# The first attention's output projection and the norm behind it, taken in two token halves that are set into the work around them

## The chip, the cores and the metric

The kernel runs on one core of one Trainium2 chip. The metric is the device time of one execution in microseconds (us). The core has a matmul engine (TensorE, PE; its weight loads are shown as PEld), VectorE (DVE), ScalarE (ACT), GpSimd (POOL) and SyncE (SP), which here issues all transfers. Each engine works through its own list of instructions strictly in order and waits on semaphores.

## The reference

Two transformer-like layers over 1024 tokens (`x`, 256 wide), cut to their structure:

```python
x = x + 0.5 * L0_ffn(layernorm(x))    # gate/up/down weights rebuilt from splines, silu(gate)*up
x = x + L0_attn(layernorm(x))         # 32 heads of 8, RoPE, banded bias, causal, softmax offset, @ Wo.T
x = x + 0.5 * L0_ffn(layernorm(x))    # the same weights again
x = x + 0.5 * L1_ffn(layernorm(x))    # ternary weights, rms norm inside
x = x + L1_attn(layernorm(x))         # 16 heads of 128 in 4 groups, causal
x = x + 0.5 * L1_ffn(layernorm(x))
return x
```

The change lies where the first attention ends and the second `L0_ffn` begins:

```python
out = einsum('bhij,bhjd->bhid', p, v) / denom[..., None]
out = out.transpose(0, 2, 1, 3).reshape(B, S, Dm)
return out @ Wo.T
```

## The kernel before

The order of work is written out by hand, once for each engine: `ffn(0)`, `qkv`, `attention`, `attention_out`, `norm(2)`, `ffn(1)`, `ffn(2)`, `grouped` (the second attention), `norm(5)`, `ffn(3)`. `X` holds the residual, tokens on partitions in eight blocks `tb`; `xn` holds the normed tokens, and during the first attention its output before the projection. `lnH` and `lnL` hold the transposed tokens as a high and a low part of float32 in a rounded format, since a product of full precision is made of three passes (`PASSES3`: high by high, high by low, low by high). PSUM has eight banks of 128 x 512 float32.

The attention takes 8 groups of 4 heads. Group g has 12 units (`UNITS2`): units 0 to 3 are for the first 512 queries, 4 to 11 for the others, each against one block of 128 keys. In a unit PE makes the scores (`look2`, L1274, in banks 2, 3, 4, 6), adds the band (`look2_bands`, L1291), makes the values of the unit before (`values`, L1311, bank 7), and ScalarE exponentiates (L936). In all groups but the last, PE also makes maxima for later groups (`look1`, L1229). After each half a group's output is copied to `oS` (`output_copy`), transposed back (`outputs`, L1320) and divided into `xn` by VectorE (L1763 to L1768). For the last group the first half's output is turned in unit 5, the second's after the last unit.

Then follows `attention_out`: all of `xn` is transposed (`transposed`, L1107, banks 0 to 3), ScalarE copies the high parts (L820), VectorE subtracts the low parts (L1602), PE makes 48 products with `WOA` (L1077), VectorE adds them to `X` (L1790). Around this stand six transpositions of the next layer's quantised weights (`quant_turn`, L1387), which ScalarE copies out. `norm(2)` takes statistics (L1578, L1581, L1583), GpSimd the power -0.5 (L696), VectorE scales (L1588), PE transposes again (L1107), and again high and low parts are made.

`ffn(1)` has 16 steps, eight for each token half: step t makes gate and up for 128 of 1024 inner features (`gate_up`, twelve products of 512 columns, banks 4 to 7) and then `down(t - 2)` (six products, L1171, banks 0 and 1 for the first half, 2 and 3 for the second). The first half needs only the first half's `lnH` and `lnL`. The hook `side` puts other work behind a step. After step 10 the first half's sum is copied out, and a norm follows that is already made by halves:

```python
                    if NORM_AFTER[f] is not None and t == AT_TURN:
                        norm_half(NORM_AFTER[f], 0)
                    if side:
                        side(t)
```

The queries of groups 1, 4 and 7 lie in the same memory as `lnH`, so `lnH` can't be written before the last group's scores are made. The transfers of the output weights of the second attention (`w_dense`, L680) wait on SP for `x_new` of the whole first attention.

## Time and profile before

| | us |
|---|---|
| median of 3 runs | 1083.94 |
| lowest, highest | 1083.74, 1088.75 |
| profiled execution, its own time | 1085.72 |
| its span, first to last instruction | 1083.9 |
| mean granted clock of PE | 0.962 of 2.4 GHz |

The profile is of one execution. The page gives sums; the timeline gives instructions in order of time, merged where the same form repeats (x16), with the idle time of the engine before it and what ended it in square brackets. Ends of matmuls are modelled: the start of the next instruction tells more than the length of one. L numbers are lines of the kernel before.

### The profile page before, as it was taken

The numbers are of one execution on the slowest core, as the hardware profiler recorded it, in microseconds if no ns is written. First come the engines' busy times: TensorE is split into PE (matmuls) and PEld (weight loads), VectorE is DVE, ScalarE is ACT, GpSimd is POOL, SyncE is SP. The second block draws the span as 40 slices with busy tenths as digits, with TensorE's granted clock in tenths as the row PEclk, the third lists the DMA queues.
The fourth block names the chain that finished last, engine by engine and source line by source line (L and its number), as shares of the span: only waits on it lengthen the run. The fifth ranks groups of instructions, "written<-read, shape, count | busy, mean of one in ns | idle before, by whom it ended". The sixth has DMA issues, their size and how long they took to land. (4 is left out here: it accounts for less than half of the span.)

```text
span 1083.9 us, 20902 instructions
## 1 busy us (share of the span) xinstructions
PE 976.4 (90%) x7872; PEld 669.5 (62%) x7896; DVE 751.0 (69%) x1865; ACT 577.4 (53%) x1167; POOL 398.9 (37%) x261
## 2 busy tenths in 40 slices
PE   4999677999999998989989879999999999999697
PEld 3787423333444343678867657777777777777585
DVE  7756976889888982254577657767777776777644
ACT  6442403666766677543355446555556555555264
POOL 3011220045423550000045036555656555566155
PEclk9999857999999999989989999999999999999899
DMA  4020434235532401022010000000000000000001
GB/s 108 1 81 27 153 66 85 45 71 95 97 71 62 95 23 60 1 78 78 1 40 0 1 1 1 2 1 2 2 2 2 2 2 2 1 2 2 1 1 40
DMA packets 25182, 37.94 MB, mean 35 GB/s; under 512 B 3000, under 2 KB 20904, under 8 KB 23560
## 3 DMA queue, kind: packets, MB, share of 16 engines
q1 hardware_dynamic: 25080, 36.59, 14.4%
q8 instruction: 63, 1.03, 0.4%
q14 instruction: 39, 0.32, 0.1%
HBM read 30.53 MB, written 5.85 MB: 34 GB/s over the span
## 5 line engine op out<-in xcount | busy, mean ns | idle before, releaser
L812 POOL TENSOR_SCALAR P<-P,rec 128x1024 f32<-128x1024 f32 (+7 forms) x128 | 220.1, 1724 | 177.2 <-DVE rec L1858 177.2
L936 ACT ACTIVATE PT<-bank 128x512 f32<-128x512 f32 (+2 forms) x320 | 153.0, 552 | 86.8 <-PE bank L1291 80.4
L1717 DVE CUSTOM_DVE_ANT_0 bank<-bank,stripS 128x128 f32<-128x128 f32 (+1 forms) x224 | 129.3, 606 | 29.3 <-PE bank L1229 29.3
L1443 PE MATMUL pair<-KH,QH 128*128 128x512 f16 (+3 forms) x576 | 116.1, 329 | 16.5 <-ACT P L1005 13.8
L1005 ACT ACTIVATE P<-pair,nm 128x1024 f32<-128x1024 f32 (+7 forms) x128 | 95.5, 746 | 56.0 <-DVE nm L1837 56.0
L1484 PE MATMUL bank<-PT,VH 128*128 128x128 f16 x1728 | 117.2, 219 | 0.1
L1229 PE MATMUL bank<-KT,QT 96*128 96x128 bf16 (+1 forms) x336 | 104.4, 338 | 10.5 <-DVE MX L1717 5.4
L1484 PEld LDWEIGHTS bank<-PT,VH 128*128 128x128 f16 x1728 | 107.0, 98 | 2.9 <-DVE PT L1866 0.2
L1866 DVE TENSOR_TENSOR PT<-bank,PT 128x384 f16<-128x384 f32 (+1 forms) x192 | 99.7, 547 | 11.6 <-ACT PT L820 11.6
L1274 PE MATMUL bank<-QT,KT 128*128 128x512 bf16 (+3 forms) x360 | 93.2, 326 | 13.7 <-ACT PT L936 5.6
L1632 DVE TENSOR_TENSOR hf<-sil,bank 128x512 f32<-128x512 f32 x64 | 44.0, 687 | 88.8 <-PE bank L1077 66.1
L1833 DVE TENSOR_REDUCE mx<-pair 128x1 f32<-128x1024 f32 (+7 forms) x128 | 95.8, 748 | 10.7 <-PE pair L1445 10.7
L820 ACT ACTIVATE PT<-bank 128x384 f16<-128x384 f32 (+1 forms) x192 | 86.6, 488 | 18.0 <-PE bank L1472 17.1
L696 POOL TENSOR_TENSOR rstd<-veps,mhalf 128x4 f32<-128x4 f32 x12 | 12.7, 1061 | 225.9 <-DVE veps L1583 225.9
L1472 PE MATMUL bank<-ident,P 128*128 128x128 f32 x576 | 85.7, 275 | 5.6 <-POOL P L812 5.3
L861 ACT ACTIVATE sil<-bank 128x512 f32<-128x512 f32 x64 | 38.3, 598 | 97.8 <-PE bank L1077 97.4
L1077 PE MATMUL bank<-lnH,W 128*128 128x512 f32 x256 | 86.7, 401 | 3.0 <-DVE W L1570 3.0
L1229 PEld LDWEIGHTS bank<-KT,QT 96*128 96x128 bf16 x336 | 29.2, 98 | 89.0 <-DVE MX L1717 47.2
L1443 PEld LDWEIGHTS pair<-KH,QH 128*128 128x128 f16 x576 | 47.6, 98 | 56.3 <-ACT P L1005 24.5
L1311 PE MATMUL bank<-PT,V 128*32 128x512 f32 (+3 forms) x768 | 79.6, 489 | 0.3 <-ACT PT L936 0.3
L1472 PEld LDWEIGHTS bank<-ident,P 128*128 128x128 f32 x576 | 64.6, 141 | 17.4 <-POOL P L812 8.4
L1274 PEld LDWEIGHTS bank<-QT,KT 128*128 128x128 bf16 x384 | 34.3, 98 | 53.6 <-ACT PT L936 33.4
(181 smaller groups left out, 1951.1 us busy)
## 6 DMA issues: line engine op xcount, KB each, us to landing
KT<-qk_dram SPq DMA_DIRECT2D x21, 192.0 KB
stripS<-band_rows SPq DMA_DIRECT2D x28, 128.0 KB, 3.0
qk_dram<-parts SPq DMA_DIRECT2D x12, 256.0 KB, 2.3
stripT<-seq_dram SPq DMA_DIRECT2D x27, 88.0 KB, 8.6
q_raw<-w_gu SPq DMA_DIRECT2D x4, 512.0 KB, 10.7
w_raw<-w_dense SPq DMA_DIRECT2D x2, 1024.0 KB, 7.0
w_raw<-w_q SPq DMA_DIRECT2D x2, 1024.0 KB, 5.5
QT<-qk_dram SPq DMA_DIRECT2D x14, 128.0 KB
```

What stands on the lines that cost most here:

```text
L812: pool.tensor_scalar(rows, rows, rec1[:, m % 4:m % 4 + 1], None, ALU.mult).then_inc(s["pn"], 1)
L936: act.activation(PT[:, n % 4, hs[0]:hs[-1] + 1, 0:ni], src, ACT.Exp).then_inc(s["s2_exp"], 1)
L1005: act.activation(P1[:, n % 3, 0:P * (ib + 1)], pair[n % 2][:, 0:P * (ib + 1)], ACT.Exp, bias=nm1[:, n % 2:n % 2 + 1], scale=SCALE1, accum_ ...
L1077: ins = pe.matmul(out, lhs(l, k), rhs(r, k), start=first and i == 0, stop=last and i == len(todo) - 1)
L1229: pe.matmul(ring_bank(use)[:, 0:nj], queries(g)[0:ROWS, h, P * ib:P * (ib + 1)], KT3[0:ROWS, g % 3, h, j0:j0 + nj], start=True, stop=True) ...
L1274: ins = pe.matmul(score_bank(i2)[:, ni * j:ni * (j + 1)], KT3[:, g % 3, h, P * jb:P * (jb + 1)], queries(g)[:, h, i0:i0 + ni], start=(j == ...
L1443: ins = pe.matmul(out, QH1[:, h % 2, l, P * ib:P * (ib + 1)], KH1[:, r, h // (H1 // GR), HALF * c:HALF * c + nj], start=(i == 0), stop=(i ...
L1472: ins = pe.transpose(rt_bank(use)[:, P * b:P * (b + 1)], P1[:, m % 3, HALF * c + P * b:HALF * c + P * (b + 1)], ident)
L1484: ins = pe.matmul(to, VH1[:, l, jb, DH * grp:DH * (grp + 1)], PT1[:, m % 3, r, P * jb:P * (jb + 1)], start=(jb == 0 and i == 0), stop=(jb ...
L1717: dve.tensor_tensor_reduce(out, out, stripS[:, h, HALF - nj:HALF], 1.0, LOWEST, ALU.add, ALU.max, mx).then_inc(s["s1_max"], 1)
L1833: dve.tensor_reduce(mx1[:, n % 2:n % 2 + 1], pair[n % 2][:, 0:P * (ib + 1)], AX_X, ALU.max).then_inc(s["sc_mx"], 1)
L1866: dve.tensor_tensor(PT1[:, m % 3, 1, cols], rt_bank(use)[:, 0:P * nb], PT1[:, m % 3, 0, cols], ALU.subtract).then_inc(s["tp_lo"], 1)
```

## The change

The work between the last exponentials and `ffn(1)` is cut by token halves. First half: its `xn` is transposed in the last group after unit 6's scores and values, into banks 0 and 1, and its high and low parts go to `AH` and `AL` (memory of the keys of two groups that are done); 24 products with `WOA` follow in unit 7 (banks 5 and 0); VectorE adds, takes statistics in unit 7 and scales in unit 8; PE transposes for the norm after unit 11, ahead of the last values. `ffn(1)` then starts. Second half, behind its steps: step 0 the last `outputs` (bank 3), step 1 the transposition (banks 2 and 3), step 2 the 24 products, step 3 the scaling, step 4 the norm's transposition; the quantised weights are turned at steps 5 (two), 6, 7, 8 and 9, in banks 2 and 3, which `down(8)` needs from step 10 on. ScalarE's and VectorE's `layer1_weights` go from steps 3 and 6 to 5 and 8, and from 4 and 7 to 6 and 9. `lnH` is still written only after the last scores.

```diff
         stripS = z("stripS", [P, GH, HALF], F32)
+        AH, AL = (Zone(zone_kt + 2 * GH * S * i)(f"A{i}", [P, KT, S], F32R) for i in (0, 2))
         stripT = z("stripT", [ROWS, 2, GH, STRIP], BF16)
...
-        QUANT_BANKS = [6, 7, 0, 1, 2, 3]
+        OUT_BANKS = [5, 0, 2, 3]
+        QUANT_AT = {5: (0, 1), 6: (2,), 7: (3,), 8: (4,), 9: (5,)}
+        def a_turn(half):
+            return 8 + 4 * half
+        def n_turn(half):
+            return 10 + 4 * half
         QUANT_OPS = 8
...
                 RING += [("s", i, 0) for i in look1_at(g, u)] + ([turn(g, u)] if turn(g, u) else [])
-        RING += [("o", NG - 1, 1)]
         at_ring = {u: i for i, u in enumerate(RING)}
...
         def ring_bank(use):
+            if use == ("o", NG - 1, 1):
+                return bank[3]
             if use[0:2] == ("m", 0):
...
+            def turned(out, at, half):
+                for hh in range(2):
+                    act.wait_ge(s["ln_tr"], at + hh + 1)
+                    copy(out[:, hh, HALF * half:HALF * (half + 1)], bank[2 * half + hh]).then_inc(s["ln_hi"], 1)
             def transposed(i, halves=(0, 1)):
...
                             signs(g)
+                        if g == NG - 1 and u == 6:
+                            turned(AH, a_turn(0), 0)
+                turned(lnH, n_turn(0), 0)
                 output_copy(NU * NG)
...
             qkv()
+            def beside_ffn1(t):
+                if t == 1:
+                    turned(AH, a_turn(1), 1)
+                if t == 4:
+                    turned(lnH, n_turn(1), 1)
+                if t in (5, 8):
+                    layer1_weights((t - 5) // 3)
+                for c in QUANT_AT.get(t, ()):
+                    quant_out(c)
             attention()
-            transposed(2)
-            for c in range(6):
-                quant_out(c)
-            transposed(3)
-            ffn(1, side=lambda t: layer1_weights(t // 3 - 1) if t in (3, 6) else None)
+            ffn(1, side=beside_ffn1)
             finish(1, 1)
...
                     if t % MT == 0:
-                        pe.wait_ge(s["ln_lo"], 4 * TR_OF_SUB[n] + 2 * tc + 2)
+                        pe.wait_ge(s["ln_lo"], n_turn(tc) + 2 if f == 1 else 4 * TR_OF_SUB[n] + 2 * tc + 2)
+                    if f == 1 and t == 0:
+                        pe.wait_ge(s["s2_exp"], N2 * NG)
+                    if f == 1 and t == 1:
+                        pe.wait_ge(s["acc_ev"], 2 * NG)
+                        pe.wait_ge(s["x_new"], TB + 2)
                     for m, (b, name, freed) in enumerate(((4, "gate", "silu"), (6, "up", "h"))):
...
                     pe.wait_ge(s["hlo"], base + t + 1)
+                    if f == 1 and t == MT:
+                        pe.wait_ge(s["q_ev"], 6)
                     if f == 0 and t < MT and t % 2 == 0:
...
                 pe.wait_ge(s["acc_ev"], 2 * g + w + 1)
-                wait_ring(pe, use)
+                if use in at_ring:
+                    wait_ring(pe, use)
+                else:
+                    pe.wait_ge(s["s2_exp"], N2 * NG)
                 for b in range(4):
...
                         transposition(turn(g, u))
+                        if g == NG - 1 and u == 6:
+                            attention_turn(0)
+                        if g == NG - 1 and u == 7:
+                            attention_out(0)
+                norm_half(2, 0)
                 values(NU * NG - 1)
-                outputs(NG - 1, 1)
-            def attention_out():
-                pe.wait_ge(s["on"], 2 * NG)
-                for th in range(2):
-                    transposed(th)
-                quant_turn(0, 2)
-                pe.wait_ge(s["ln_lo"], 4 * 2 + 4)
-                for tb in range(TB):
-                    if tb == 4:
-                        pe.wait_ge(s["q_ev"], 2)
-                    ins = products(bank[4 + tb // 2][:, D * (tb % 2):D * (tb % 2 + 1)], lambda p, k: ln(p, k, P * tb, P),
+            def attention_turn(half):
+                pe.wait_ge(s["on"], 2 * NG - 1 + half)
+                pe.wait_ge(s["s1_max"], len(LOOK1))
+                pe.wait_ge(s["m_ev"], 2 * NG)
+                transposed(half)
+            def attention_out(half):
+                pe.wait_ge(s["ln_lo"], a_turn(half) + 2)
+                for tb in range(4 * half, 4 * half + 4):
+                    ins = products(bank[OUT_BANKS[tb // 2]][:, D * (tb % 2):D * (tb % 2 + 1)], lambda p, k: (AH, AL)[p][:, k, P * tb:P * (tb + 1)],
                                    lambda p, k: WOA[:, p, k, :], PASSES3)
...
-            def quant_turn(first, last):
-                if first == 0:
+            def quant_turn(c):
+                if c == 0:
                     pe.wait_ge(s["q_in"], 16)
-                    pe.wait_ge(s["acc_ev"], 2 * NG)
-                for c in range(first, last):
-                    dst = bank[QUANT_BANKS[c]].bitcast(BF16)
-                    for b in range(8):
-
-                        src = q_keep[:, c, D * (b % 4) + P * (b // 4):D * (b % 4) + P * (b // 4 + 1)] if c < 4 else q_keep[:, c, P * b:P * (b + 1)]
-                        ins = pe.transpose(dst[:, P * b:P * (b + 1)], src, identb[:, :])
-                    ins.then_inc(s["q_tr"], 1)
+                    pe.wait_ge(s["ln_lo"], n_turn(1) + 2)
+                if c >= 2:
+                    pe.wait_ge(s["q_ev"], c - 1)
+                dst = bank[2 + c % 2].bitcast(BF16)
+                for b in range(8):
+                    src = q_keep[:, c, D * (b % 4) + P * (b // 4):D * (b % 4) + P * (b // 4 + 1)] if c < 4 else q_keep[:, c, P * b:P * (b + 1)]
+                    ins = pe.transpose(dst[:, P * b:P * (b + 1)], src, identb[:, :])
+                ins.then_inc(s["q_tr"], 1)
+            def beside_ffn1(t):
+                if t == 0:
+                    outputs(NG - 1, 1)
+                if t == 1:
+                    attention_turn(1)
+                if t == 2:
+                    attention_out(1)
+                if t == 4:
+                    norm_half(2, 1)
+                for c in QUANT_AT.get(t, ()):
+                    quant_turn(c)
...
             attention()
-            attention_out()
-            quant_turn(2, 6)
-            pe.wait_ge(s["q_ev"], 6)
-            norm(2)
-            ffn(1)
+            ffn(1, side=beside_ffn1)
             ffn(2, side=beside_ffn2)
...
+            def turned(hi, lo, at, half):
+                cols = slice(HALF * half, HALF * (half + 1))
+                for hh in range(2):
+                    dve.wait_ge(s["ln_hi"], at + hh + 1)
+                    dve.tensor_tensor(lo[:, hh, cols], bank[2 * half + hh], hi[:, hh, cols].bitcast(F32), ALU.subtract).then_inc(s["ln_lo"], 1)
             def rms(f, tc):
...
                             group_sums(g - 1)
-                outputs(NG - 1, 1)
+                        if g == NG - 1 and u == 6:
+                            turned(AH, AL, a_turn(0), 0)
+                        if g == NG - 1 and u == 7:
+                            attention_out(0)
+                            norm_stats(2, 0)
+                        if g == NG - 1 and u == 8:
+                            norm_apply(2, 0)
+                turned(lnH, lnL, n_turn(0), 0)
-            def attention_out():
-                transposed(2)
-                for tb in range(TB):
+            def beside_ffn1(t):
+                if t == 0:
+                    outputs(NG - 1, 1)
+                if t == 1:
+                    turned(AH, AL, a_turn(1), 1)
+                if t == 2:
+                    attention_out(1)
+                    norm_stats(2, 1)
+                if t == 3:
+                    norm_apply(2, 1)
+                if t == 4:
+                    turned(lnH, lnL, n_turn(1), 1)
+                if t in (6, 9):
+                    layer1_weights(t // 3 - 2)
+            def attention_out(half):
+                for tb in range(4 * half, 4 * half + 4):
                     dve.wait_ge(s["wo_mm"], tb // 2 + 1)
-                    dve.tensor_tensor(X[:, tb, :], bank[4 + tb // 2][:, D * (tb % 2):D * (tb % 2 + 1)], X[:, tb, :], ALU.add).then_inc(s["x_new"], 1)
+                    dve.tensor_tensor(X[:, tb, :], bank[OUT_BANKS[tb // 2]][:, D * (tb % 2):D * (tb % 2 + 1)], X[:, tb, :], ALU.add).then_inc(s["x_new"], 1)
...
             attention()
-            attention_out()
-            norm(2)
-            ffn(1, side=lambda t: layer1_weights(t // 3 - 1) if t in (4, 7) else None)
+            ffn(1, side=beside_ffn1)
             ffn(2, side=beside_ffn2)
```

How the instructions stand now. PE in the last group, before: two units' scores (L1274), bands (L1291) and values (L1311), from the scores of unit 6 on.

```order
L1274 MATMUL bank<-QT_121,KT_92 128x512 x4
L1311 MATMUL bank<-PT,V_94 32x512 x4
L1274 MATMUL bank<-QT_121,KT_92 128x512 x4
L1291 MATMUL bank<-stripT,flipb 32x128 x16
L1311 MATMUL bank<-PT,V_94 32x512 x4
L1274 MATMUL bank<-QT_121,KT_92 128x512 x4
L1291 MATMUL bank<-stripT,flipb 32x256 x16
```

PE in the same place, with the change (scores L1305, bands L1322, values L1342).

```order
L1305 MATMUL bank<-QT_123,KT_92 128x512 x4
L1342 MATMUL bank<-PT,V_94 32x512 x4
L1131 MATMUL bank<-ident,xn 128x128 x8
L1305 MATMUL bank<-QT_123,KT_92 128x512 x4
L1322 MATMUL bank<-stripT,flipb 32x128 x16
L1342 MATMUL bank<-PT,V_94 32x512 x4
L1101 MATMUL bank<-WOA,A_99 128x256 x2
L1101 MATMUL bank<-WOA,A_100 128x256
...
L1305 MATMUL bank<-QT_123,KT_92 128x512 x4
L1322 MATMUL bank<-stripT,flipb 32x256 x16
```

Eight transposes of `xn` stand ahead of unit 7's scores, and behind unit 7's values 24 products with `A` (written as x2 and x1 rows, the first pair of eight is shown) ahead of unit 8's scores; the last two rows are unit 8's scores and bands.

ScalarE from the group's last exponentials to the first steps of the block, before.

```order
L936 ACTIVATE PT<-bank 128x2x256 x2
L936 ACTIVATE PT<-bank 128x2x128 x2
L820 ACTIVATE oS<-bank 128x512
L820 ACTIVATE lnH<-bank 128x512 x4
L820 ACTIVATE WGU_68<-bank 128x2x512 x4
L820 ACTIVATE WD_69<-bank 128x8x128 x2
L820 ACTIVATE lnH<-bank 128x512 x4
L861 ACT_TABLE_LOAD
L861 ACTIVATE sil<-bank 128x512 x2
```

ScalarE there, with the change (exponentials L951, copies L829, silu L876).

```order
L951 ACTIVATE PT<-bank 128x2x256 x2
L951 ACTIVATE PT<-bank 128x2x128 x2
L829 ACTIVATE lnH<-bank 128x512 x2
L829 ACTIVATE oS<-bank 128x512
L876 ACT_TABLE_LOAD
L876 ACTIVATE sil<-bank 128x512 x2
L829 ACTIVATE hH<-hf 128x512
L829 ACTIVATE A_99<-bank 128x512 x2
L876 ACTIVATE sil<-bank 128x512
```

The copies that stood between the exponentials and the first silu have gone, but for two of `lnH` and one of `oS`; two copies of `A` now follow the second silu.

VectorE between the attention and the block, before: low parts, additions to `X`, statistics, scalings, low parts.

```order
L1602 TENSOR_TENSOR lnL<-bank,lnH 128x512 x4
L1790 TENSOR_TENSOR X<-bank,X 128x256 x8
L1578 BN_STATS stats<-X 128x6 x4
L1581 BN_AGGR mv<-stats 128x2 x4
L1583 TENSOR_SCALAR veps<-mv 128x4
L1578 BN_STATS stats<-X 128x6 x4
L1581 BN_AGGR mv<-stats 128x2 x4
L1583 TENSOR_SCALAR veps<-mv 128x4
L1588 TENSOR_SCALAR xn<-X,mv,rstd 128x256 x8
L1602 TENSOR_TENSOR lnL<-bank,lnH 128x512 x4
```

VectorE with the change, steps 0 to 2 of the block (`hf` and `hL` are the block's own, L1686 and L1692).

```order
L1686 TENSOR_TENSOR hf<-sil,bank 128x512
L1817 TENSOR_TENSOR DEN<-bank,EO 128x16
L1819 RECIPROCAL REC<-DEN 128x16
L1822 TENSOR_TENSOR xn<-bank,REC 128x4x32
L1686 TENSOR_TENSOR hf<-sil,bank 128x512
L1692 TENSOR_TENSOR hL<-hf,hH 128x512
L1656 TENSOR_TENSOR A_100<-bank,A_99 128x512 x2
L1686 TENSOR_TENSOR hf<-sil,bank 128x512
L1692 TENSOR_TENSOR hL<-hf,hH 128x512
L1865 TENSOR_TENSOR X<-bank,X 128x256 x4
L1625 BN_STATS stats<-X 128x6 x4
L1628 BN_AGGR mv<-stats 128x2 x4
```

The division of the last output stands behind step 0, the low parts of `A` behind step 1, and the additions to `X` with the second half's statistics behind step 2.

## Rows read from the trace of the kernel before

**Rows 1.** The page: busy us (share of the span) xinstructions of each engine.

```profile
PE 976.4 (90%) x7872; PEld 669.5 (62%) x7896; DVE 751.0 (69%) x1865; ACT 577.4 (53%) x1167; POOL 398.9 (37%) x261
```

**Rows 2.** Busy time by engine in three stretches; the column before DMA is the granted clock.

```profile
core 0: us, PE busy (x) PEld busy (x) DVE busy (x) ACT busy (x) POOL busy (x), PEclk, DMA share, GB/s
427.90:445.90 18.00, 16.17 (x185) 5.96 (x183) 0.72 (x3) 14.36 (x30) 0.00 (x0) 1.00 0.00 1
445.90:468.20 22.30, 16.70 (x140) 15.71 (x140) 14.07 (x43) 10.39 (x14) 2.28 (x2) 0.80 0.30 95
468.20:534.80 66.60, 66.60 (x300) 55.03 (x298) 31.27 (x54) 25.54 (x41) 1.01 (x1) 0.99 0.09 32
```

**Rows 3.** Timeline (start us, us, engine, line), last group, units 7 and 8.

```profile
435.70 0.41 PE L1291 MATMUL bank<-stripT,flipb 96*32 96x128 bf16 x16
...
435.94 1.03 PE L1311 MATMUL bank<-PT,V 128*32 128x512 f32 x8
436.05 2.06 ACT L936 ACTIVATE PT<-bank 128x512 f32<-128x512 f32 x4 [0.73 <-PE bank L1291]
...
437.19 1.37 PE L1274 MATMUL bank<-QT,KT 128*128 128x512 bf16 x3 [0.22 <-ACT PT L936]
...
438.49 0.62 PE L1291 MATMUL bank<-stripT,flipb 96*32 96x256 bf16 x16
```

**Rows 4.** Timeline from the last exponentials to the second feed-forward block.

```profile
445.00 0.61 PE L1311 MATMUL bank<-PT,V 128*32 128x256 f32 x8
445.17 0.66 ACT L936 ACTIVATE PT<-bank 128x256 f32<-128x256 f32 x2 [0.34 <-PE bank L1291]
...
448.57 3.09 PE L1107 MATMUL bank<-ident,xn 128*128 128x128 f32 x16 [0.88 <-DVE xn L1768]
...
453.07 0.50 PE L1077 MATMUL bank<-WOA,lnH 128*128 128x256 f32 x2
...
458.92 1.96 PE L1387 MATMUL bank<-identb,q_keep 128*128 128x128 bf16 x32
...
461.74 1.04 POOL L696 TENSOR_TENSOR rstd<-veps,mhalf 128x4 f32<-128x4 f32 x1 [56.36 <-DVE veps L1583]
...
463.36 2.83 DVE L1588 TENSOR_SCALAR xn<-X,mv,rstd 128x256 f32<-128x256 f32 x8
...
464.88 3.65 PE L1107 MATMUL bank<-ident,xn 128*128 128x128 f32 x16 [4.00 <-DVE xn L1588]
...
468.23 0.79 PE L1077 MATMUL bank<-lnH,W 128*128 128x512 f32 x1
```

**Rows 5.** The granted clock by the microsecond.

```profile
449.00:450.00 1.00, 1.00 (x9) 1.00 (x7) 0.11 (x1) 0.61 (x2) 0.00 (x0) 0.61 0.00 0
452.00:453.00 1.00, 1.00 (x13) 0.90 (x11) 0.84 (x2) 0.74 (x2) 0.00 (x0) 0.68 0.00 0
...
462.00:463.00 1.00, 0.00 (x0) 0.00 (x0) 1.00 (x5) 1.00 (x2) 0.78 (x1) 0.94 0.96 316
...
469.00:470.00 1.00, 1.00 (x5) 0.76 (x4) 0.72 (x2) 0.98 (x2) 0.00 (x0) 0.65 0.00 0
```

**Rows 6.** Timeline, eight transposes set into feed-forward work at full clock.

```profile
519.39 1.03 PE L1136 MATMUL bank<-ident,OT 128*128 128x128 f32 x8
...
520.18 0.47 PE L1077 MATMUL bank<-lnH,W 128*128 128x512 f32 x1
...
532.56 1.04 PE L1107 MATMUL bank<-ident,xn 128*128 128x128 f32 x8
...
533.83 1.29 DVE L1602 TENSOR_TENSOR lnL<-bank,lnH 128x512 fp32r<-128x512 f32 x2 [1.09 <-ACT lnH L820]
```

**Rows 7.** Timeline of PE, second block, starts of steps 3 and 4.

```profile
478.59 0.39 PE L1077 MATMUL bank<-lnH,W 128*128 128x512 f32 x1
...
482.67 0.39 PE L1077 MATMUL bank<-lnH,W 128*128 128x512 f32 x1
```

**Rows 8.** Busy time and clock while the attention starts up.

```profile
145.00:176.00 31.00, 23.31 (x128) 7.38 (x125) 23.45 (x53) 4.06 (x6) 0.00 (x0) 0.50 0.18 33
```

2 lines of the change are left out of this document (1 added, 1 removed).

## The prediction

> **What bounds the kernel now.** I read the page's totals first, then the stretch that the change touches, then its timeline. TensorE (PE) is busy 976.4 of 1083.9 us [rows 1], so the time is PE's own work plus the 107 us in which it stands still, plus what it loses when its clock is at the lower level. A change that keeps every matmul, as this one does, can gain only from the last two.
>
> The touched stretch lies in three parts [rows 2]. In the last group's units 4 to 11 (18.0 us) PE is busy 16.2. From the last exponentials to the second feed-forward block (22.3 us) it is busy 16.7: 5.6 us are idle, and the mean granted clock is 0.80. In the block itself (66.6 us) it is busy all the time: whatever is put in there is paid in full, but nothing waits as long as other engines have their parts ready.
>
> The middle part in order of time [rows 4]: the last exponentials start at 445.17 and take 0.66, so they end at 445.83. Then come sixteen transposes (448.57, 3.09 us), two hand-over transpositions of the quantised weights, 48 output products (453.07 to 458.92), four more weight transpositions (1.96 us), then 4.0 us of waiting for the norm, sixteen transposes (3.65 us), and the block's first product at 468.23. The clock drops to 1.2 GHz twice (a granted clock of 0.50, which shows as 0.61, 0.68, 0.94 and 0.65 in the microseconds in which it changes) [rows 5]. A value v in such a microsecond means that the share 2(1 - v) of it was slow; so the first drop begins at 449.2 and ends at 452.6, the second begins near 462.9 and ends at 469.7. Of the second, about 1.4 us already lie in the block. I take this out: steps 3 and 4 start at 478.59 and 482.67, 4.08 us apart for 18 products, 0.227 each [rows 7]. Before step 3 the block has issued 42 products, 9.5 us at that rate, so at full clock it would have started at 469.05. **The stretch to replace is 469.05 - 445.83 = 23.2 us.**
>
> **The change part by part.** Matmuls and transposes of full width keep their number and shapes; only one wait on PE is removed as such (for all six weight transpositions, ahead of the norm). So I price the new order in three sums.
>
> *a. What is put into the last group.* After unit 6's scores come eight transposes, in unit 7 24 output products. At full clock eight such transposes take 0.79 (519.39 to 520.18) [rows 6]. A product of 256 columns takes (458.92 - 453.07)/48 = 0.122 [rows 4], so 24 take 2.9. With about 0.3 for two seams between forms that is 4.0 us. What can hide it: one unit's bands start at 435.70, the next unit's at 438.49, a cycle of 2.8 us in which ScalarE's four exponentials (2.06) and PE's scores take turns [rows 3]. PE waits 0.22 ahead of the next scores and its three products take 1.37 where three unhindered ones take about 0.7. So about 0.6 of a cycle is free; only the unit with the products can use it, since the transposes sit between values and scores where PE follows a release. The group gets 4.0 - 0.6 = **3.4 us** longer. Bounds: 4.0 if nothing hides, 2.8 if both insertions use the slack. ScalarE's two copies and VectorE's two subtractions (a chain of 2.56 from the first transpose to the last subtraction: 532.56 to 533.83 + 1.29) [rows 6] stand ahead of unit 7's exponentials and of its products. The transposes (0.8), scores (0.9), bands (0.4) and the values (1.0) pass meanwhile, 3.1 us, so the chain is covered by half a microsecond; if that cover went, the products would wait and unit 8 with them.
>
> *b. The hand-over of the first half.* It starts as soon as the values of unit 10 are through (445.00 + 0.61, that is 0.2 before the last exponentials end) [rows 4]: eight transposes, copy, subtraction, 2.56 us, and 0.1 to the first product. The last values (0.4) and the exponentials lie beside it. The block then starts 2.56 - 0.2 + 0.1 = **2.5 us** after the last exponentials. Is the norm's first half ready? From the end of the products to GpSimd's power took 461.74 - 458.92 = 2.8, the power takes 1.04, four of the eight scalings (2.83) take 1.4 [rows 4]: 5.3 us with the seams. Units 8 to 11, from the end of unit 7's products to the last values, take 438.49 to 445.61 plus the scores ahead, 8 us. Spare: 2.7 us.
>
> *c. What is put into the block.* Four output transposes 0.5 (half of 0.79, and a seam), twice eight transposes 0.9 each with seam, 24 products 3.0, and the 48 weight transposes: 1.96/32 = 0.061 each, 2.9, with six seams 3.5. Sum 0.5 + 1.8 + 3.0 + 3.5 = **8.8 us**, nothing hidden. Bounds: 7.9 with no seams at all; 11 if the transposes fall into slow clock (3.65 for sixteen instead of 1.6). Does PE wait there? The output transposes come after step 0; VectorE's three operations on them are done in under 1 us, while step 1's twelve products last 2.7. The second half's turn comes after step 1, its products after step 2 (4.1 us later, against a chain of 2.56). The norm after that needs 5.3 us and is asked for after all of steps 3 and 4 (8.2 us). VectorE waits at step 2 for the products, with the next product of the gate behind it, but that one is ready only 2.7 us later. Each weight transposition has a whole step for its ScalarE copy. The loads of the next layer's output weights on the SP queue wait for the second half's residual and start later against the block, yet they are needed only after the third block. So I cost all of these at nothing; their cover is 1.5 to 3 us each.
>
> Sum: 23.2 - (3.4 + 2.5 + 8.8) = **8.5 us gained**. The profiled execution took 1085.72 with a span of 1083.9; I forecast 1077.2 with a span of 1075.4. The median of the three runs, 1083.94, is 1.8 below the profiled one, so the median goes to **1075.4 us**. From ends that add up: 10.7 gained at best, 3 at worst with slow clock and no slack.
>
> **The rivals.**
>
> *R1: slow clock at the hand-over.* Between the end of unit 11's scores and the block PE has eight transposes, short values and about 1.4 us of waiting. The two drops came after such stretches (the second after 2 us idle) [rows 4, 5]. If it falls there, the transposes cost 0.8 more, the values 0.4, and 1.4 us of the block pass at half rate (0.7): 1.9 us, **1077.3**. Against it: the idle piece is a third of the one before the second drop, and dense products follow. The Trainium skill, "TensorE: Matmul & The Clock Gate", Part 4: PE-mode transpose, says that transposes do not count as activity for the clock; by that rule this hand-over would be nearly all idle and this rival the forecast. The trace disagrees: the clock rose at 452.6 when nothing but transposes had run since 448.57 [rows 4, 5]. Chance 0.18.
>
> *R2: the last group pays more.* ScalarE is what times the cycle; if its two copies (0.6 each) come late for unit 7 and unit 7's products wait for the low parts, the slack is not used (0.6), the copies are paid (1.2), and one set of exponentials (2.06 us [rows 3]) no longer lies beside PE's work: 3.8 us, **1079.2**. For it: the chain's cover is only half a microsecond. Chance 0.12.
>
> *R3: the change doesn't do what it says.* The second half's chain is as long as the first's, and PE stands before it in the block as it did outside: the 5.6 us idle come back, **1081.0**. For it: PE, ScalarE and VectorE each work strictly in order, and each now holds a wait for another in steps 1, 2 and 4. Against it: the covers above. Chance 0.05.
>
> *R4: slower.* The clock, once down at the hand-over, stays down through the block's first steps, where products are broken by transposes and waits. In this program it was down from 145 to 176 though PE was busy 23.3 of 31.0 us [rows 8]. The same 31 us at half rate in the new stretch lose 15.5: 1075.4 + 15.5 = **1090.9**. It decides from 17 us at 1.2 GHz on, where the loss equals the gain. Against it: the block before released the clock 1.4 us after its first product. Chance 0.05.
>
> *R5: more is gained.* Seams cost nothing (0.9 back), both insertions in the group use the slack (0.6), and the 1.4 us of waiting at the hand-over vanish: 2.9 us more, **1072.5**. Chance 0.10.
>
> **How the numbers follow.** The forecast keeps 0.50. A measurement of this kernel tells 0.5% from no change, 5.4 us, so faster means below 1078.5: the forecast, R1 and R5, 0.78. Within 0.5%: R2 and R3, 0.17. Slower: R4, 0.05. The range from 1072.8 to 1080.0 holds the forecast, R1, R2 and half of R5, 0.85, and the bounds of sums a and c.
>
> **What would show it.** In the changed profile: transposes and products inside the last group, whose end moves by 3.4 us (last exponentials ending near 449.2); the block's first product near 451.7; PE busy without gaps to the block's end, with steps 0 to 9 stretched by 8.8 in all; no granted clock of 0.5 after 449. The gap of 4.0 us before the norm's transposes is gone. The forecast is wrong if PE waits inside the block by more than 1 us in sum, if units 7 and 8 stretch by more than 5, or if the clock falls at the hand-over.

## The result, and the profile after

The changed kernel takes 1079.03 us in the median of six runs (1077.57 to 1079.93). The kernel before, run beside it and counted with the three runs shown ahead, has a median of 1088.45 over six (1083.74 to 1089.55). The ratio is 0.9929, 95% interval [0.9912, 0.9946]: 7.7 us faster (5.9 to 9.6), which is more than the 0.5% that can be told from no change; the two medians themselves lie 9.4 apart. The profiled execution took 1078.95 us with a span of 1076.9. The forecast of 1075.4 is 3.6 too low, but inside the stretch that it priced the trace comes out close to it.

The page's totals: the span is 7.0 shorter, and PE's busy time the same as before [rows 1] to 0.1. That sameness says little: before's count lacks 24 matmul records (x7872 against x7896), and PE ran slowly for 3.4 us near 424 in this execution and not in that one (below). The stretch further down has equal counts and shows the difference.

```profile
PE 976.3 (91%) x7896; PEld 664.9 (62%) x7896; DVE 750.6 (70%) x1865; ACT 577.3 (54%) x1167; POOL 399.2 (37%) x261
```

Busy time in the three parts of the stretch, with PE's granted clock ahead of the DMA share, after:

```profile
core 0: us, PE busy (x) PEld busy (x) DVE busy (x) ACT busy (x) POOL busy (x), PEclk, DMA share, GB/s
435.00:451.40 16.40, 16.12 (x189) 8.60 (x188) 6.76 (x22) 10.81 (x23) 1.04 (x1) 1.00 0.00 1
451.40:453.70 2.30, 1.12 (x16) 0.68 (x13) 1.29 (x2) 1.92 (x4) 0.00 (x0) 1.00 0.04 7
453.70:530.50 76.80, 75.98 (x396) 62.79 (x397) 38.58 (x77) 32.66 (x49) 2.02 (x2) 1.00 0.16 55
```

Against [rows 2] (whose first row starts two units earlier): the middle part, 22.3 us before, is 2.3; the block behind it is longer, because it now holds the second half; the clock is 1.00 in all three, where it was 0.80 and 0.99 in the last two.

PE's timeline after, last group from unit 6's scores, and the hand-over:

```profile
435.05 1.03 PE L1305 MATMUL bank<-QT,KT 128*128 128x512 bf16 x4
...
437.00 1.09 PE L1131 MATMUL bank<-ident,xn 128*128 128x128 f32 x8
...
440.09 3.13 PE L1101 MATMUL bank<-WOA,A 128*128 128x256 f32 x24
...
450.54 0.61 PE L1342 MATMUL bank<-PT,V 128*32 128x256 f32 x8
451.07 1.09 PE L1131 MATMUL bank<-ident,xn 128*128 128x128 f32 x8
452.10 0.42 PE L1342 MATMUL bank<-PT,V 128*32 128x128 f32 x8
453.74 0.50 PE L1101 MATMUL bank<-lnH,W 128*128 128x512 f32 x1 [1.22 <-DVE lnL L1656]
...
456.61 0.60 PE L1354 MATMUL bank<-ident,oS 128*128 128x128 f32 x4
```

The first half's transposes (437.00) and 24 products (440.09) stand in the group; behind unit 11's bands come eight transposes, the last values, 1.22 us of waiting, and the block. Behind the block's step 0 come the four transposes of the last outputs (456.61). The other two engines at the same place, after:

```profile
439.24 2.07 ACT L951 ACTIVATE PT<-bank 128x512 f32<-128x512 f32 x4 [0.46 <-PE bank L1322]
...
444.43 2.07 ACT L951 ACTIVATE PT<-bank 128x512 f32<-128x512 f32 x4 [3.12 <-PE bank L1322]
...
447.09 1.39 DVE L1635 TENSOR_SCALAR xn<-X,mv,rstd 128x256 f32<-128x256 f32 x4 [1.16 <-POOL rstd L705]
...
450.71 0.66 ACT L951 ACTIVATE PT<-bank 128x256 f32<-128x256 f32 x2 [0.34 <-PE bank L1322]
...
452.40 1.29 DVE L1656 TENSOR_TENSOR lnL<-bank,lnH 128x512 fp32r<-128x512 f32 x2 [3.92 <-ACT lnH L829]
```

ScalarE's exponentials of unit 7 (439.24) and unit 8 (444.43) are 3.12 us of idling apart: that is the place of the 24 products. The norm's scaling (447.09 to 448.5) is done 2.6 us before PE turns its result (451.07). The last exponentials end at 450.71 + 0.66 = 451.37.

PE's waits in the block, up to the third block's first weight product, after:

```profile
engine line waited for: us in total, times, longest us
PE bank L1101 <- DVE lnL L1656: 1.2, 1, 1.2
PE bank L1202 <- DVE hL L1692: 0.8, 1, 0.8
```

The first is the wait at the hand-over; the second, 0.8, is there before too, at 535.77. Nothing waits behind the second half's steps. Four landmarks bring the two spans together. "Stretch" runs from unit 6's scores in the last group to the third block's first product; "rest" is from there to the end of the span.

| | unit 6's scores | last exponentials end | second block starts | third block's first product | stretch | rest | span |
|---|---|---|---|---|---|---|---|
| before | 432.78 | 445.83 | 469.05 (at full clock) | 537.26 | 104.5 | 546.6 | 1083.9 |
| after | 435.05 | 451.37 | 453.74 | 530.53 | 95.5 | 546.4 | 1076.9 |

The stretch gains 9.0 us; what lies ahead of it, where the two kernels are alike, lost 2.3; the rest gained 0.3. The whole stretch in one row each, before and then after:

```profile
432.80:537.30 104.50, 97.12 (x598) 76.48 (x597) 46.97 (x101) 45.58 (x75) 3.29 (x3) 0.95 0.12 41
```

```profile
435.10:530.50 95.40, 93.12 (x598) 71.99 (x596) 46.63 (x101) 45.29 (x75) 3.06 (x3) 1.00 0.13 45
```

The same 598 matmul instructions. PE stood still for 7.4 us before and 2.3 after, which is 5.1 of the gain; it was busy for 97.1 and 93.1, which is the other 4.0. That part is clock: 0.95 means that a tenth of 104.5 us went at 1.2 GHz, and it is all gone. In the two slow pieces of before, 449.2 to 452.6 and 462.9 to 469.7 [rows 5], PE is busy for 8.2 us, which at half rate loses 4.1.

### The profile page after: what moved, and what is told of

Its sections match the earlier page's. It is cut to its first block, busy times and chain, and to the rows that moved or that the text cites. A ratio compares the mean times of both kernels' runs of the same rounds, so it can differ in the third digit from the quotient of the medians.

```text
span 1076.9 us, 20929 instructions
## 1 busy us (share of the span) xinstructions
PE 976.3 (91%) x7896; PEld 664.9 (62%) x7896; DVE 750.6 (70%) x1865; ACT 577.3 (54%) x1167; POOL 399.2 (37%) x261
## 4 chain that ended last, share of the span: by engine, by line
PE 32%; DVE 8%; issue 5%; ACT 3%; POOL 2%; ACTq 0%; DVEq 0%
PE bank L1101 14%; PE pair L1494 7%; PE bank L1535 3%; PE bank L1523 3%; DVE mx L1908 3%; PE bank L1202 2%; POOL P L821 2%; ACT QH L829 1%; ACT P L1023 1%; DVE xn L1635 1%; PE bank L1131 1%; DVE CT L1950 1%; DVE stats L1625 0%; DVE hL L1692 0%; DVE WQ L1877 0%
## 5 line engine op out<-in xcount | busy, mean ns | idle before, releaser
L951 ACT ACTIVATE PT<-bank 128x512 f32<-128x512 f32 (+2 forms) x320 | 153.0, 552 | 91.1 <-PE bank L1322 84.5
L1023 ACT ACTIVATE P<-pair,nm 128x1024 f32<-128x1024 f32 (+7 forms) x128 | 95.5, 746 | 56.1 <-DVE nm L1912 56.0
L1535 PEld LDWEIGHTS bank<-PT,VH 128*128 128x128 f16 x1728 | 107.0, 98 | 2.9 <-DVE PT L1941 0.2
L1305 PE MATMUL bank<-QT,KT 128*128 128x512 bf16 (+3 forms) x384 | 99.1, 333 | 10.6 <-ACT PT L951 5.1
L1686 DVE TENSOR_TENSOR hf<-sil,bank 128x512 f32<-128x512 f32 x64 | 44.0, 687 | 87.1 <-PE bank L1101 57.4
L1908 DVE TENSOR_REDUCE mx<-pair 128x1 f32<-128x1024 f32 (+7 forms) x128 | 95.8, 749 | 10.7 <-PE pair L1496 10.7
L829 ACT ACTIVATE PT<-bank 128x384 f16<-128x384 f32 (+1 forms) x192 | 86.6, 488 | 18.0 <-PE bank L1523 17.1
L705 POOL TENSOR_TENSOR rstd<-veps,mhalf 128x4 f32<-128x4 f32 x12 | 12.5, 1043 | 218.9 <-DVE veps L1630 218.9
L876 ACT ACTIVATE sil<-bank 128x512 f32<-128x512 f32 x64 | 38.3, 599 | 89.1 <-PE bank L1101 88.7
L1342 PE MATMUL bank<-PT,V 128*32 128x512 f32 (+3 forms) x768 | 80.5, 494 | 0.0
```

What stands on the lines that cost most here:

```text
L951: act.activation(PT[:, n % 4, hs[0]:hs[-1] + 1, 0:ni], src, ACT.Exp).then_inc(s["s2_exp"], 1)
L1023: act.activation(P1[:, n % 3, 0:P * (ib + 1)], pair[n % 2][:, 0:P * (ib + 1)], ACT.Exp, bias=nm1[:, n % 2:n % 2 + 1], scale=SCALE1, accum_ ...
L1305: ins = pe.matmul(score_bank(i2)[:, ni * j:ni * (j + 1)], KT3[:, g % 3, h, P * jb:P * (jb + 1)], queries(g)[:, h, i0:i0 + ni], start=(j == ...
L1535: ins = pe.matmul(to, VH1[:, l, jb, DH * grp:DH * (grp + 1)], PT1[:, m % 3, r, P * jb:P * (jb + 1)], start=(jb == 0 and i == 0), stop=(jb ...
L1908: dve.tensor_reduce(mx1[:, n % 2:n % 2 + 1], pair[n % 2][:, 0:P * (ib + 1)], AX_X, ALU.max).then_inc(s["sc_mx"], 1)
```

## Experiments: the same two kernels again

Theory: local sums a, b and c are right, and the miss lies in the level from which they were taken. Rival: the change itself costs 2 to 3 us somewhere outside the stretch. The changed kernel and the kernel before, each unaltered, once more.

> The changed kernel again, unaltered, beside the kernel before on one chip. I measure two things: the time, and the local stretch from the start of unit 6's scores in the last group to the first product with WGU1 in the third feed-forward block (before 537.26 - 432.78 = 104.5 us, changed 530.53 - 435.05 = 95.5). Theory (the local sum holds, what lies ahead of the last group scatters between executions by some us with the moment at which the clock is released): the stretch is 95.5 within 0.2 again, the scores of unit 6 start anywhere from 432 to 436, and the ratio of times is 0.990 to 0.993 (8 to 11 us). Rival (the change costs time elsewhere, ahead of the last group or after the block): unit 6's scores start at 435 again while the kernel before would start them at 432.8, and the ratio is 0.993 to 0.995.

> The kernel before, unaltered, for a second profile. Theory (local sum fixed, the rest scatters with the moment at which the clock is released near 177): the stretch from unit 6's scores to the third block's first product is 104.5 within 0.3, unit 6's scores start between 432 and 436, later by about 1 us for each us by which the release is later than 176. Rival (what lies ahead of the last group is itself different in the two kernels): its scores start at 432.8 again whatever the release.

e1: 1077.21 us (1073.25 to 1077.86), ratio 0.9902 [0.9885, 0.9918] to a median of 1087.37 over 17 runs of before (1083.17 to 1090.19). Its landmarks: 432.79, 449.12, 451.49, 528.28; stretch 95.5, rest 543.2, span 1071.5. e9, a single execution: 1088.32 us, beside eleven others of before with a median of 1085.58 (1083.15 to 1089.38); unit 6's scores at 434.36, stretch 104.4, rest 546.7, span 1085.5. So the stretch repeats to 0.1 us for either kernel, while what lies ahead of it moves by 2.3 in e1 and by 1.6 in e9, and the rest by 3.2 in e1, with nothing altered. The miss is not the change's. Where do the two come from?

**Ahead of the stretch** it is a drop of the clock near 424, in the first units of the last group, which only some executions have. The same eight products (values of one unit), before and e1, then e9 and the changed kernel:

```profile
423.58 1.03 PE L1311 MATMUL bank<-PT,V 128*32 128x512 f32 x8
423.60 1.03 PE L1342 MATMUL bank<-PT,V 128*32 128x512 f32 x8
```

```profile
423.53 1.90 PE L1311 MATMUL bank<-PT,V 128*32 128x512 f32 x8
424.23 1.93 PE L1342 MATMUL bank<-PT,V 128*32 128x512 f32 x8
```

The clock in that microsecond, before and then e9:

```profile
424.00:425.00 1.00, 1.00 (x12) 0.45 (x5) 0.00 (x0) 1.00 (x4) 0.00 (x0) 1.00 0.00 0
```

```profile
424.00:425.00 1.00, 1.00 (x8) 0.00 (x0) 0.00 (x0) 1.00 (x3) 0.00 (x0) 0.50 0.00 0
```

In e9 and after the clock is down for 3.4 us from here on; in before and e1 it stays at 1.00. At 423.5 e9 is level with before to 0.05 us, and at unit 6's scores it is 1.6 later: the drop is all of it. After is 0.6 behind e1 at 423.6 (424.23 - 423.60) and 2.3 at the scores, so 1.6 of its 2.3 are the same drop. Ahead of the place stand four short waits of PE for ScalarE, 0.49, 0.15, 0.64 and 0.15 us in after; e1 has them too (0.51, 0.15, 0.64, 0.15) and kept its clock.

Another reading offers itself, and it is the one that the expectations of e1 and e9 start from: the microsecond in which the clock comes back after the long slow piece [rows 8]. Before, e9 and the changed kernel:

```profile
176.00:177.00 1.00, 1.00 (x9) 0.34 (x5) 0.47 (x1) 1.00 (x3) 0.00 (x0) 0.92 1.23 203
```

```profile
177.00:178.00 1.00, 1.00 (x6) 0.46 (x4) 0.67 (x3) 0.03 (x1) 0.00 (x0) 0.60 1.14 99
```

```profile
178.00:179.00 1.00, 1.00 (x12) 0.46 (x14) 0.63 (x4) 0.00 (x0) 0.00 (x0) 0.77 0.80 96
```

Counted as in the prediction, the clock came back at 176.2 (before), 176.7 (e1), 177.8 (e9) and 178.5 (after), and unit 6's scores followed in that order. But e9, whose clock came back 1.6 us after before's, was level with it at 423.5, so the late return by itself delayed nothing there. e9's expectation, 1 us later for each us, is met in its number and not in its mechanism. What goes with the return is the drop: of the 13 profiles of this case the six with a return up to 177.47 (before, e1, e4, e6, e7, e11) have none near 424, the seven from 177.54 on (after, e2, e3, e5, e8, e9, e10) have it. What ties the two together no run shows.

**In the rest** it is whether PE's clock survives waits that are there in every run. PE's timeline, third block, first wait, before and then after; then a wait in the second attention, after and then e1:

```profile
551.54 0.75 PE L1171 MATMUL bank<-hH,WD 128*128 128x512 f32 x1 [2.00 <-DVE hL L1638]
```

```profile
544.80 0.50 PE L1202 MATMUL bank<-hH,WD 128*128 128x512 f32 x1 [2.01 <-DVE hL L1692]
```

```profile
625.69 2.42 PE L1494 MATMUL pair<-KH,QH 128*128 128x512 f16 x6 [2.52 <-ACT P L1023]
```

```profile
621.78 1.31 PE L1494 MATMUL pair<-KH,QH 128*128 128x512 f16 x6 [2.52 <-ACT P L1023]
```

The same wait of 2.0 us is followed by a product of 0.75 us in one run and of 0.50 in another; the same 2.52 us by six products in 2.42 us or in 1.31, in one and the same kernel. Before had such a drop at the third block's first wait and at its second (1.98 us, 564.50), after at the second alone (1.97 us, 556.21). The clock about these two waits, before and then after (e1 shows 1.00 for both):

```profile
547.30:557.30 10.00, 8.00 (x32) 6.42 (x31) 7.82 (x9) 4.69 (x7) 3.65 (x3) 0.83 0.00 0
557.30:567.30 10.00, 8.02 (x31) 6.14 (x30) 8.06 (x7) 5.15 (x10) 5.75 (x3) 0.90 0.33 107
```

```profile
540.50:550.50 10.00, 7.99 (x40) 6.35 (x39) 8.32 (x11) 6.15 (x10) 3.72 (x3) 1.00 0.00 1
550.50:560.50 10.00, 8.03 (x29) 6.03 (x28) 7.44 (x7) 5.07 (x10) 5.76 (x3) 0.84 0.28 107
```

From the third block's first product to its second wait takes 564.50 - 537.26 = 27.2 us before, 25.7 after and in e1: one drop costs 1.5 to 1.6. From the third block to the second attention e1 has no such drop, after two (556.21, 625.69) and before three (551.54, 564.50, 633.95). After's two are the 3.2 by which its rest exceeds e1's. Before's three cost 4.6 (by the starts of ScalarE's instructions against e1's), but it is only 3.4 above e1: it gets back 1.1, most of it at the very end, where its clock falls for the last time 3.2 us ahead of the end of the span, against 7.3 in e1 and 7.6 in after. The Trainium skill, "TensorE: Matmul & The Clock Gate", Part 1, says of a kernel's start that the number of matmuls at the lower clock varies from run to run of one kernel. These rows, 550 us and more into the kernel, show the same kind of variation.

## Experiments: the clock's share of what went away

The changed order removes 5.1 us of standing still and 4.0 of slow work. Theory: of the two drops, the second (at the norm's wait) is worth 1.6 to 2 by itself. e3 takes the kernel before and fills the 4 us ahead of the norm with sixteen products whose result nobody reads:

```diff
+        FILL = 16
...
             quant_turn(2, 6)
+            pe.wait_ge(s["x_new"], TB + 2)
+            for i in range(FILL):
+                pe.matmul(bank[4], W0[:, 0, 0, P * (i % 8):P * (i % 8 + 1)], lnH[:, 0, 0:HALF], start=True, stop=True)
             pe.wait_ge(s["q_ev"], 6)
```

> The kernel before, with 16 dummy products of 512 columns (3.6 us, result unused) in the 4.0 us in which PE waits for the norm. If slow clock is a part of what the change saves, as my sum has it (transposes and the block's first products at 1.2 GHz): no granted clock of 0.5 after 453, the second block's effective start comes about 1.6 to 2 us earlier, the stretch shrinks from 104.5 to about 102.7, time 1.6 to 2 us less. If only the idle time counts (rival): the stretch stays at 104.5 within 0.3, since the wait itself is not shortened.

1085.19 us (1082.81 to 1088.91), 0.9985 [0.9969, 1.0001]; stretch 103.4, so 1.1 less than before, between the theory's 1.8 and its rival's 0. In time it is 1.6 us faster, with an interval that includes no change. PE's timeline, e3:

```profile
463.78 3.90 PE L1512 MATMUL bank<-lnH,W 128*128 128x512 f32 x16
467.98 1.07 PE L1108 MATMUL bank<-ident,xn 128*128 128x128 f32 x8 [0.30 <-DVE xn L1592]
469.35 1.09 PE L1108 MATMUL bank<-ident,xn 128*128 128x128 f32 x8 [0.30 <-DVE xn L1592]
470.62 0.50 PE L1078 MATMUL bank<-lnH,W 128*128 128x512 f32 x1 [0.18 <-DVE lnL L1606]
```

The transposes take 1.07 and 1.09 where they took 3.65 [rows 4], so the clock is up. But then they wait 0.30 for each half of `xn` and the block 0.18 for the low part: with the clock up, VectorE's scaling is what ends last, and it gives back 0.8. The clock alone is worth little there; the idle time must go as well.

e6 and e10 go the other way, on the changed kernel: the wait at the hand-over made longer, by doing VectorE's subtractions for the first half twice (e10: only the first of the two, its condition is `at == n_turn(0) and hh == 0`).

```diff
                     dve.wait_ge(s["ln_hi"], at + hh + 1)
+                    if at == n_turn(0):
+                        dve.tensor_tensor(lo[:, hh, cols], bank[2 * half + hh], hi[:, hh, cols].bitcast(F32), ALU.subtract).then_inc(s["twice"], 1)
+                        dve.wait_ge(s["twice"], hh + 1)
```

> The changed kernel with VectorE's two low-part subtractions at the hand-over each made twice, so that PE's wait ahead of the block grows from 1.2 to about 2.6 us. If the gap costs what it lasts: the stretch is 95.5 + 1.4 = 96.9 and the granted clock stays 1.00. If a longer gap drops the clock, as in the kernel before after 2 us idle: a granted clock of 0.5 for some 3 us behind it and a stretch of 98.3 to 99.

> Only the first of the two subtractions at the hand-over made twice: PE's wait grows from 1.2 to about 2.0 us. If the clock falls only for the longer wait: stretch 95.5 + 0.7 = 96.2 and clock 1.00. If it falls at 2 us already: 97.7 and about 3 us at 0.50.

e6: 1079.27 us (1076.26 to 1080.63), 0.9921 [0.9902, 0.9941]; wait 2.67, stretch 98.4. e10, a single execution: 1078.15 us; wait 1.94, stretch 97.8. Against the changed kernel e6 loses 2.9 us for 1.45 of waiting, e10 2.3 for 0.72. The surplus is 1.5 to 1.6 us both times: one drop of the clock, priced as in the third block. In time e6 is 2.1 us slower than e1 (1077.21). e10's block start, then its clock, by the microsecond:

```profile
454.84 0.67 PE L1101 MATMUL bank<-lnH,W 128*128 128x512 f32 x1 [1.94 <-DVE lnL L1659]
```

```profile
455.00:456.00 1.00, 1.00 (x3) 0.81 (x4) 0.00 (x0) 0.02 (x1) 0.00 (x0) 0.51 0.00 0
...
458.00:459.00 1.00, 1.00 (x5) 0.81 (x4) 0.00 (x0) 0.28 (x1) 0.00 (x0) 0.79 0.00 0
```

So rival R1 of the prediction is real, and its size (1.9) was about right, though not by its terms: in e10 the eight transposes and the last values take 1.09 and 0.43, as at full clock, and the loss is the 3.4 us of the block at half rate (1.7), where R1 had 1.2 for the former and 0.7 for the block. It did not come in the three profiles with the wait of 1.2 us (after, e1, e7), but 0.7 us more brought it.

## Experiments: one half of the change undone

Theory: the gain comes from having other work beside each half's chain. e4 keeps the second half inside the block but does the first half's transposes, products and norm after the last scores instead of in units 6 to 8. e5 keeps the first half inside the group and does the second half's whole chain ahead of the block. The edits on PE (ScalarE's and VectorE's follow them), e4 and then e5, whose four calls in `beside_ffn1` go:

```diff
-                        if g == NG - 1 and u == 6:
-                            attention_turn(0)
-                        if g == NG - 1 and u == 7:
-                            attention_out(0)
-                norm_half(2, 0)
+                attention_turn(0)
                 values(NU * NG - 1)
+                attention_out(0)
+                norm_half(2, 0)
```

```diff
                 values(NU * NG - 1)
+                outputs(NG - 1, 1)
+                attention_turn(1)
+                attention_out(1)
+                norm_half(2, 1)
```

> The changed kernel with the first half's part taken out of the last group and set behind it (transposes, 24 products, norm, hand-over, one after another); the second half stays in the block. Theory (what pays is that each half's chain has other work beside it): the last group shrinks by 3.3 us to 13.05 from unit 6's scores to the last exponentials, but the block starts 13 us behind these instead of 2.4, with a wait of about 5 us for the norm in it and a granted clock of 0.5 behind that: stretch 95.5 - 3.3 + 10.8 + 1.5 for clock = 104.5, as long as in the kernel before, ratio 0.998 to 1.000. Rival (the gain is in the second half inside the block, the last group's part only shifts work): the stretch stays below 98.

> The changed kernel with the second half's outputs, transposes, products and norm transposes taken out of the block and set ahead of it (the quantised weights stay at steps 5 to 9). Theory: the block starts 14 to 15 us behind the last exponentials instead of 2.4, is 5.2 us shorter, and loses 1.5 us to the clock after a wait of about 5 us: stretch 95.5 + 12 - 5.2 + 1.5 = 103.8 within 1, ratio 0.997 to 1.000. Rival (only the first half's place matters): stretch below 98.

e4: 1087.37 us (1083.86 to 1088.90), 0.9993 [0.9980, 1.0007] to a before of 1087.22. e5: 1088.27 (1086.06 to 1090.76), 1.0005 [0.9992, 1.0019]. Either half undone takes away the whole gain. The longest waits of PE from the last exponentials to the block (what waited, for what: us, times, longest), e4 and then e5:

```profile
PE bank L1130 <- DVE xn L1632: 5.3, 1, 5.3
PE bank L1100 <- DVE lnL L1653: 1.4, 1, 1.4
PE bank L1100 <- DVE A L1653: 1.2, 1, 1.2
```

```profile
PE bank L1129 <- DVE xn L1629: 5.3, 1, 5.3
PE bank L1099 <- DVE A L1650: 1.6, 1, 1.6
```

The chain from the output products over the statistics, GpSimd's power and the scaling to the norm's transposes holds PE for 5.3 us each time it has nothing beside it: the 5.3 us that the prediction worked out for it. e4's stretch is 105.5 (expected 104.5); e5's is 107.0, and there the expectation of 103.8, give or take 1, failed by 3.2. It had 1.5 in it for one drop of the clock. The rows in which the clock changes, e5:

```profile
457.00:458.00 1.00, 0.68 (x5) 0.68 (x6) 0.27 (x1) 0.00 (x0) 0.00 (x0) 0.97 0.02 8
...
461.00:462.00 1.00, 0.97 (x7) 0.76 (x5) 0.00 (x0) 0.00 (x0) 0.00 (x0) 0.82 0.00 0
...
464.00:465.00 1.00, 0.00 (x0) 0.00 (x0) 0.65 (x6) 0.00 (x0) 0.23 (x1) 0.88 0.75 166
...
471.00:472.00 1.00, 1.00 (x4) 0.76 (x4) 0.00 (x0) 0.37 (x2) 0.00 (x0) 0.70 0.00 0
```

The clock falls twice, once on the 24 products (457.32, which take 4.65 us where the same 24 take 3.13 at 440.09 after), once on the norm's transposes and the block's start. By these rows that is 457.9 to 461.4 and 464.8 to 471.6, 3.4 + 6.8 us at half rate. PE is busy for 3.4 and 4.3 of these, which loses up to 3.9, 2.4 more than the 1.5 that was expected. The other 0.8 of the 3.2 isn't accounted for; PE's waits ahead of the 24 products (0.87, 0.88 and 1.57 us) lie in that part.

## Experiments: is more to be had?

e2 puts the hand-over's transposes ahead of unit 11's bands, so that VectorE's low parts are ready when the last values end; e11 adds that the weights are turned in pairs, with two seams fewer; e7 sets products without use ahead of the waits at 125 to 150, to keep the clock up there; e8 is e2 and e7. e2 on PE (ScalarE's `turned(lnH, n_turn(0), 0)` goes ahead of unit 11's exponentials), what e11 adds, and e7 in `look1_pair` (`keep_clock(n)` is n products into bank 4):

```diff
+                        if g == NG - 1 and u == NU - 1:
+                            norm_half(2, 0)
                         look2_bands(g, u)
...
-                norm_half(2, 0)
                 values(NU * NG - 1)
```

```diff
-        QUANT_AT = {5: (0, 1), 6: (2,), 7: (3,), 8: (4,), 9: (5,)}
+        QUANT_AT = {5: (0, 1), 7: (2, 3), 9: (4, 5)}
```

```diff
                 if n == 0:
+                    pe.wait_ge(s["v9"], TB // 4)
+                    keep_clock(14)
                     pe.wait_ge(qk_first, 16 * 8)
...
                 if n == 2 * 4:
+                    keep_clock(8)
                     pe.wait_ge(qk_in[0], 16 * 8)
```

> The changed kernel with the first half's norm transposes set between unit 11's scores and bands, and ScalarE's two copies of lnH ahead of the last exponentials. If the chain of transposes, copies and subtractions (2.56 us) alone sets the start of the block: the block starts about 0.6 us earlier against unit 6's scores (18.7 in the changed kernel, 18.0 here), and the stretch to the third block shrinks from 95.5 to 94.8; the time by 0.6 us, too little to tell from the changed kernel. If instead the last exponentials and values set it (they are pushed back by the copies, 1.1 us): the start stays at 18.7 or later.

> The early turn of the second experiment, and the quantised weights turned in pairs at steps 5, 7 and 9 instead of at 5, 6, 7, 8 and 9. If a seam between forms costs PE 0.1 us, as my sum of 8.8 for the block has it: two seams fewer, stretch 94.7 - 0.2 = 94.5. If the pair waits for ScalarE's copies or holds up the second half's down products at step 10: 95 or more.

> The changed kernel with dummy products (14 and 8 of 512 columns, results unused) in the two waits of PE for transfers where the first attention starts, around 125 and 139 us. In all profiles so far the clock is at 0.50 from 129 to between 176 and 178.5, and the scores of unit 6 start the later the later it is released (432.8 at 176.0, 435.5 at 178.5). If this stage is bound by PE at slow clock: with the clock kept up it ends earlier, unit 6's scores start at 425 to 430, and the time falls by 4 us or more; the local stretch stays 95.5. If VectorE (busy 23.5 of 31 us there) or the transfers bound it: unit 6's scores start within 432 to 436 and only the scatter may shrink.

> The early turn (second experiment) and the dummy products at the attention's start in one kernel. If each does what it does alone: local stretch 94.7, unit 6's scores where the kernel with the dummy products alone has them, and a time 0.7 us below that one.

| | median us (range) | ratio to before [95%] | stretch |
|---|---|---|---|
| e2 | 1075.92 (1074.20 to 1077.29) | 0.9899 [0.9882, 0.9916] | 94.7 |
| e11 | 1076.23 (1074.17 to 1079.62) | 0.9909 [0.9887, 0.9932] | 94.5 |
| e7 | 1075.86 (1072.65 to 1076.77) | 0.9883 [0.9865, 0.9902] | 95.5 |
| e8 | 1076.50 (1073.70 to 1077.14) | 0.9896 [0.9880, 0.9913] | 94.7 |

In the stretch e2 wins 0.8 us, as expected, and e11 0.3 more; in time all four agree with e1 (0.9902) within their intervals. e8 was expected 0.7 below e7 and came out 0.6 above it, within the scatter; its scores began at 434.15, not at e7's 432.14, with the drop near 424 that e7 lacks. For e7 two windows of the start of the attention:

```profile
145.00:150.00 5.00, 4.06 (x37) 1.04 (x36) 5.00 (x6) 0.00 (x0) 0.00 (x0) 1.00 0.56 90
...
155.00:160.00 5.00, 4.66 (x25) 0.92 (x23) 4.82 (x6) 0.66 (x2) 0.00 (x0) 0.50 0.01 2
```

The products kept the clock up until 131.8 and brought it back from 142.0 to 152.3; then it was down again until 176.2. So some 14 of about 48 slow us are gone, and unit 6's scores come at 432.14 against 432.79 in e1: 0.65 us, not the 3 to 8 that PE as the bound would give. Where the clock is up, VectorE is busy for 5.00 of 5 us and PE for 4.06, which speaks for VectorE as what sets the pace there. From 152 to 176 e7 left the clock as it was, so about that part it says nothing.

## Why the prediction was right, and where it failed

- **The stretch to replace, 23.2 us**: the sum around it came out at 9.0 gained against 8.5.
- **a, 3.4**: last exponentials less unit 6's scores, 451.37 - 435.05 = 16.32, against 13.05 before: 3.3. Chain and cover held; no product waited for its low part. In e1, whose unit 6 starts where it did before, the last exponentials end at 449.12 and the block starts at 451.49, against 449.2 and 451.7 forecast.
- **b, 2.5**: 453.74 - 451.37 = 2.4.
- **c, 8.8**: 530.53 - 453.74 = 76.8, against 537.26 - 469.05 = 68.2: 8.6. No wait in steps 0 to 9; all the covers of 1.5 to 3 us held, which also settles R3.
- **R1**: did not come, but 0.7 us more of waiting would have brought it (e10). Its sign was right, its size too, though by other terms (above), and a chance of 0.18 was not too much. Of the two reasons given against it, the shortness of the idle piece fits (1.22 us kept the clock, 1.94 lost it); that dense products follow does not protect, since they followed in e6 and e10 too.
- **R2, R5**: the group paid 3.3, not 3.8 and more; seams were not free.
- **R4**: did not come. Even where the clock dropped at the hand-over (e6, e10), dense products had it back after 3.4 us.
- **The step that failed** is the one behind the sum, the level from which it is taken: "The median of the three runs, 1083.94, is 1.8 below the profiled one, so the median goes to 1075.4". Of those three runs two lay at the bottom of the kernel's spread; the 17 and 19 runs of before on later chips have medians of 1087.37 and 1087.22. Eleven more on a third chip have 1085.58. The level was taken 1.6 to 4.5 us too low (against the 1088.45 beside the result: 4.5), and the 3.6 by which the forecast missed is of that size. From 1087.4 the same sum gives 1078.9. The prediction's own line for "faster", 1078.5, hangs on the same level and sits too low with it. The profiled execution, 1085.72, was also below the middle of most of these, and the forecast from it, 1077.2, would have missed by 1.8. The change itself was sized well: 8.5 forecast, 7.7 (5.9 to 9.6) measured here and 10.7 (8.9 to 12.5) in e1.
- **Why the level spreads**: by the clock, as far as the runs show. Over the 17 runs of before beside e1 the span is 1081.2 to 1081.7 at a mean granted clock of 0.965, 1083.9 to 1086.2 at 0.962 and 1086.4 to 1088.4 at 0.959 to 0.961. From 0.965 to 0.959 is 1.2% of the span more at half rate, an estimate of 13 us, which loses up to 6.5 where PE is busy. That is four drops of 1.6. The sum had no term for how many of them the three runs happened to have.

What stays open: why the clock comes back at 176.2 in one run and 178.5 in the next, why a late return goes with a drop near 424, and why the clock survives a wait of 2.0 or 2.5 us in one run and not in another. No run here shows what decides that. How often a wait of 1.2 us costs a drop isn't known either: three profiles showed none.

## What to carry to other kernels

Split a serial chain by token halves in order to put other work beside each half; here either half left bare gave back all of the gain (e4, e5). A chain that is split and has nothing beside either half wasn't run. Price such a move per matmul at the clock of the place where it goes, and look for a second gain in the clock, here 4.0 us beside 5.1 of removed waits, since each removed wait of about 2 us and more also removes its chance of a drop (1.6 us each). And take the level of a forecast from many runs: three runs of a kernel that spreads by 5 to 7 us on one chip can miss its level by as much as half of the gain that is forecast.

## What the runs showed of the hardware

- One wait of 1.94 or 2.67 us brought the lower clock (e10, e6), one of 1.22 us didn't (after, e4). Short ones in a row came before a drop as well: 0.87, 0.88 and 1.57 us in e5; 0.49, 0.15, 0.64 and 0.15 us ahead of 424 in after, though the same row left the clock at 1.00 in e1. Waits of 2.0 and 2.52 us went either way in the same order of work. The Trainium skill, "TensorE: Matmul & The Clock Gate", Part 4, says that the full clock doesn't engage for transposes; before's rise at 452.6 behind nothing but transposes [rows 4, 5] disagrees, as the prediction had it. After doesn't test the rule: eight transposes (451.07) and values of 0.42 us lay between the bands and the wait, and the clock stayed at 1.00 to the block and through it.
- Two executions of one kernel, level to 0.05 us at 423.5 (before and e9), were 1.6 us apart 9 us later, by one drop of the clock of 3.4 us. About the same size, 1.4 to 1.7 us, turned up at each such drop over dense work in this case: at the hand-over (e6, e10), in the third block and in the second attention.
